# Gathered statistics of a second image spread over 60 attention units, and the second moments and tile mask split between the attention and the head of the convolution

## The reference

```python
x = x + _L0_conv_ref(_gn(x), W_qkv, W_out, rel_height, rel_width)  # window attention
x = x + _L1_conv_ref(_gn(x), weight, bias)                         # 3x3 convolution

def _gn(v, G=32, eps=1e-5):        # mean and variance over 4 channels and a whole image
    ...
    return ((g - m) / jnp.sqrt(s + eps)).reshape(v.shape)

def _L1_conv_ref(x, weight, bias):
    x_sp = x * _tile_mask(x)       # a 32x32 tile counts if any channel has |x| > 1e-6 in it
    y = conv 3x3 of x_sp, padding 1
    return y + bias
```

## Time and profile before

| | |
|---|---|
| median of 3 runs | 3703.85 us (3702.18 to 3705.59) |
| the profiled execution | 3702.19 us, span 3700.4 us, granted clock 0.991 |
| PE busy | 3491.4 us, 94% |
| DVE busy | 3349.1 us, 91% |
| ACT busy | 2966.0 us, 80% |
| POOL busy | 2575.1 us, 70% |
| DMA | 464.06 MB, mean 125 GB/s |

### The profile page before, as it was taken

The page is one execution under the profiler, slowest core; times in us unless marked ns, Lnnn a source line. Parts: engine busy times, 40 slices in busy tenths (PEclk is TensorE's granted clock), DMA queues, the critical chain, the costliest instruction groups (busy, mean ns, idle before and its releaser), DMA issues. The chain is left out here.

```text
span 3700.4 us, 127356 instructions
## 1 busy us (share of the span) xinstructions
PE 3491.4 (94%) x51718; PEld 2480.6 (67%) x51718; DVE 3349.1 (91%) x5626; ACT 2966.0 (80%) x5320; POOL 2575.1 (70%) x3344
## 2 busy tenths in 40 slices
PE   0799999998999999999999999999589999999999
PEld 0587777777888888888888888888434444444444
DVE  9699999999999999999999999999789888888887
ACT  0788888887999999999999999998377777777774
POOL 1677777776777777777777777777366666666664
PEclk9999999999999999999999999999799999999999
DMA  8244544443333333333333333333244434344332
GB/s 374 79 132 133 159 134 154 148 139 105 103 103 97 94 98 103 103 97 91 101 103 103 95 91 103 103 100 83 69 160 162 154 146 154 147 154 154 154 154 83
DMA packets 492549, 464.06 MB, mean 125 GB/s; under 512 B 9664, under 2 KB 469312, under 8 KB 469440
## 3 DMA queue, kind: packets, MB, share of 16 engines
q1 hardware_dynamic: 491968, 455.92, 38.4%
HBM read 321.40 MB, written 134.48 MB: 123 GB/s over the span
## 5 line engine op out<-in xcount | busy, mean ns | idle before, releaser
L984 POOL TENSOR_TENSOR sb_tf<-sb_cf 128x1024 f32<-128x1024 f32 x256 | 609.4, 2382 | 392.2 <-DVE sb_tl L966 370.3
L450 PE MATMUL ps_t<-sb_ident,sb_d 128*108 128x128 f32 x4096 | 662.3, 284 | 6.2 <-ACT sb_pt L638 1.9
L600 DVE TENSOR_TENSOR sb_qb<-ps_q,sb_own_head 128x1024 f32<-128x1024 f32 x512 | 621.1, 1213 | 14.9 <-PE ps_q L432 14.9
L470 PEld LDWEIGHTS ps_s<-sb_kf,sb_qb 128*64 128x64 f32 x16384 | 519.1, 138 | 171.5 <-issue 162.9
L719 POOL TENSOR_TENSOR sb_erel<-sb_brel 128x288 f32<-128x288 f32 x512 | 351.5, 686 | 395.6 <-DVE sb_brel L547 394.7
L892 PE MATMUL ps_c<-sb_th,sb_wc_h 128*128 128x512 f16 x1536 | 584.3, 380 | 40.3 <-DVE sb_tl L966 40.2
L470 PE MATMUL ps_s<-sb_kf,sb_qb 128*64 128x54 f32 x16384 | 585.6, 224 | 2.4 <-DVE sb_scores L580 2.4
L892 PE MATMUL ps_c<-sb_th,sb_wc_l 128*128 128x512 f16 x1536 | 583.3, 380 | 0.0
L892 PE MATMUL ps_c<-sb_tl,sb_wc_h 128*128 128x512 f16 x1536 | 583.2, 380 | 0.0
L749 POOL TENSOR_TENSOR sb_zl<-sb_zf,sb_zh 128x396 f16<-128x396 f32 x512 | 481.1, 940 | 83.1 <-ACT sb_zh L702 83.1
L735 POOL TENSOR_TENSOR sb_prod<-sb_rel,sb_shift 128x192 f32<-128x192 f32 x1024 | 502.1, 511 | 0.0
(11 more groups left out here) (117 smaller groups left out, 8228.0 us busy)
## 6 DMA issues: line engine op xcount, KB each, us to landing
sb_xb<-rows SPq DMA_DIRECT2D x128, 780.0 KB, 6.5
sb_xc<-x SPq DMA_DIRECT2D x64, 1280.0 KB, 5.4
sb_x<-rows SPq DMA_DIRECT2D x128, 512.0 KB, 4.1
x<-sb_x SPq DMA_DIRECT2D x128, 512.0 KB, 3.3
out<-sb_oc SPq DMA_DIRECT2D x64, 1024.0 KB, 3.9
sb_abuf<-rows SPq DMA_DIRECT2D x16, 2048.0 KB, 11.7
sb_st<-rows SPq DMA_DIRECT2D x32, 1024.0 KB, 9.3
sb_raw<-wconv SPq DMA_DIRECT2D x1, 576.0 KB, 3.7
```

The lines of the kernel that those rows point to most:

```text
L450: last = pe.transpose(ps_t[0:KV, wj * 128:(wj + 1) * 128], d[:, at:at + KV], ident[:])
L470: last = pe.matmul(s_at, qb[:, qc:qc + QB], kf[:, kc:kc + KR], start=True, stop=True)
L600: dve.tensor_tensor(view(qb, 0, 128, vh * QBW + p * NW * QB, [[QB, NW], [QN, HEADS], [1, QN]]), view(ps_q, 0, 128, 0, [[QN, NW], [0, HEADS ...
L984: pool.tensor_tensor(tf[:, k * TF:(k + 1) * TF], view(cf, 0, 128, c0 + ra * W, [[2 * W, PAIRROWS], [1, W]]), view(cf, 0, 128, c0 + rb * W, ...
```

## The change

Five things are done.

1. The strip of 8 rows of the second image becomes a half strip of 4 rows (512 KB), 64 in all. Units 0 to 3 take two halves each, units 4 to 59 one each. Their loads stand at the end of SP's body, and all their `bn_stats` (two a half) at the end of VectorE's g=3.
2. The moments of the second image of x are made at u=60 instead of u=38.
3. The second moments of the first image are made in the attention, at u=70, without the five steps for the edge tables, and its tile mask and row tables at u=71, with a `partition_all_reduce` on GpSimd at g=0.
4. The zero rows around x1 are stored by SP at u=4.
5. The two blocks between attention and convolution are gone. The second moments, mask and tables of the second image are made at the convolution's start, on VectorE, with one matmul, one square root and one all-reduce; ScalarE waits for the group step before its first strip, and for the tables before the first strip of the second image.

```diff
+            HALF = WS // 2 * W
+            HALVES = H * W // HALF
+            DOUBLE = 4
+
+            def gathered(u):
+
+                if 0 <= u < DOUBLE:
+                    return (2 * u, 2 * u + 1)
+                return (u + DOUBLE,) if DOUBLE <= u < HALVES - DOUBLE else ()
+
+            MOMENTS = {HALVES - DOUBLE: 1, UNITS // B + 6: 0}
+            MASK = UNITS // B + 7
...
# SP, body u
-                    if stat is not None:
-
-                        row = settled(sp, (stat[0] + STRIPS_1) * WS + PAD)
-                        sp.wait_ge(sem["st_used"], (stat[0] + 1) * PAR)
-                        sp.dma_start(st[:, h * STW:(h + 1) * STW],
-                                     x_in[:, bass.ds(row, WS), :].rearrange("p a b -> p (a b)")
-                                     ).then_inc(st_loaded[h], 16)
                     if on(u - 3, UNITS):
...
                         sp.dma_start(view(x1, 0, 128, r * WS * UW, [[UW, WS], [1, UW]]),
                                      x_in[:, bass.ds(row, WS),
                                           UW * r:UW * r + UW]).then_inc(xr_loaded[r], 16)
+                    for k in gathered(u):
+
+                        row = H + k * (WS // 2) + PAD
+                        if k >= 2:
+                            sp.wait_ge(sem["st_used"], 2 * (k - 1))
+                        sp.dma_start(st[:, k % 2 * HALF:(k % 2 + 1) * HALF],
+                                     x_in[:, row:row + WS // 2, :].rearrange("p a b -> p (a b)")
+                                     ).then_inc(st_loaded[k % 2], 16)
+                    if u == DOUBLE:
+
+                        sp.wait_ge(sem["zeroed"], 1)
+                        for row in (0, ROWS + 1):
+                            sp.dma_start(x1_dram[:, row:row + 1, :].rearrange("p a b -> p (a b)"), zrow[:]
+                                         ).then_inc(sem["edges"], 16)
...
# VectorE, body u, end of group g
-                        if stat is not None:
-                            if g != 1:
-                                stat_pieces(stat, h, (0, 4, 1, 2)[g], (1, 0, 1, 2)[g])
...
+                        if g == 3:
+                            for k in gathered(u):
+                                dve.wait_ge(st_loaded[k % 2], (k // 2 + 1) * 16)
+                                for c in range(2):
+                                    at = UNITS * 6 + (2 * k + c) * 6
+                                    dve.bn_stats(stats[:, at:at + 6],
+                                                 st[:, k % 2 * HALF + c * 512:k % 2 * HALF + (c + 1) * 512]
+                                                 ).then_inc(sem["st_used"], 1)
+                        if u in MOMENTS:
+                            b = MOMENTS[u]
+                            if g == 0:
+                                moments_sums(dve, link[b], (b,), gn_sem[b]["agg_done"])
+                            if g == 2:
+                                moments_tables(dve, link[b], (b,), gn_sem[b]["sqrt_done"], edges=(b == 1))
+                        if u == MASK and g == 0:
+                            tile_extremes(dve, link[0], 0)
+                            dve.tensor_copy(ext[1][:, 0:1], ext[0][:, 0:1]).then_inc(sem["tiles_done"], 1)
+                        if u == MASK and g == 2:
+                            row_tables(dve, link[0], 0, sem["all_tiles"])
...
# GpSimd, body u, end of group g
+                        if u == MASK and g == 0:
+                            pool.wait_ge(sem["tiles_done"], 1)
+                            pool.partition_all_reduce(tiles_of(tabs, 0), tiles_of(ext[0], 0), 128, RMAX
+                                                      ).then_inc(sem["all_tiles"], 1)
...
-        groupnorm_moments("gn1", (0, 1))
...
# convolution: SP no longer stores and waits for the zero rows; ScalarE
+                    if j + 2 == CSTRIPS // B:
+                        act.wait_ge(sem["step_done"], TABLE_STEPS)
...
+                act.wait_ge(sem["step_done"], GROUP_STEPS)
+                act.activation(gn[5][:, 1:2], gn[3][:, 1:2], ACT.Sqrt).then_inc(sem["sqrt_done"], 1)
# VectorE
+                link = linker(dve, sem["step_done"])
+                moments_sums(dve, link, (1,), sem["agg_done"])
                 for z in (th, tl):
...
+                moments_group(dve, link, (1,), ps_c, sem["sum_done"])
+                moments_tables(dve, link, (1,), sem["sqrt_done"], edges=False)
+                tile_extremes(dve, link, 1)
+                dve.tensor_copy(ext[1][:, 0:1], ext[0][:, 0:1]).then_inc(sem["tiles_done"], 1)
+                row_tables(dve, link, 1, sem["all_tiles"])
```

More of the change, by code:

```diff
@@ L161, in moments_tables, with tiles_of @@
                                               ALU.mult, ALU.mult))
+        ctab = sb("ctab", 3 * CSTRIPS * TC, F32)
+        dtab = sb("dtab", 3 * CSTRIPS * TC, F32)
+        nmean = sb("nmean", B, F32)
+        TR = ROWS // TILE
+        SPT = TILE // CROWS
+        ext = [sb(f"tile_ext{j}", TR * TC, F32) for j in range(2)]
+        tabs = sb("tile_abs", TR * TC, F32)
+        zrow = sb("zrow", W, F32)
+        def tiles_of(t, b):
+            return t[:, b * TR // B * TC:(b + 1) * TR // B * TC]
@@ new lines, in tile_extremes @@
+        def tile_extremes(dve, link, b):
+            hs, n = STRIPS // B, TR // B
+            for t, dst, op in ((tmax, ext[0], ALU.max), (tmin, ext[1], ALU.min)):
+                for h in range(2):
+                    link(dve.tensor_reduce(view(dst, 0, 128, b * n * TC + 4 * h, [[TC, n], [1, 4]]),
+                                           view(t, 0, 128, b * n * 8 * SPT + 4 * h, [[8 * SPT, n], [1, 4], [8, SPT]]),
+                                           AX.X, op))
+                part = tiles_of(dst, b)
+                link(dve.tensor_scalar(part, part, mean_t[:, b * hs:b * hs + 1],
+                                       rstd_t[:, STRIPS + b * hs:STRIPS + b * hs + 1], ALU.subtract, ALU.mult))
+            link(dve.scalar_tensor_tensor(tiles_of(ext[0], b), tiles_of(ext[1], b), -1.0, tiles_of(ext[0], b),
+                                          ALU.mult, ALU.max))
@@ L369, in units @@
                 for u in range(-3, UNITS + 4):
-                    body(u, u // 2, u % 4, some,
-                         (u - FIRST, (u - FIRST) // 2) if FIRST <= u < GN else None, u == GN)
+                    body(u, u // 2, u % 4, some)
             def z_at(z, slot, p, off, dims):
@@ L382, in _, with body @@
             def _(sp):
[L383 removed]
+                def body(u, s, slot, on):
                     h = slot % 2
@@ L425, in project @@
                     need(pe, sem["qb_done"], piece)
[L426 to L430, removed]
+                    if due is not None:
+                        pe.wait_ge(gn_sem[due]["agg_done"], 1)
+                        pe.matmul(ps_q[:, 0:2], gsum[:], aggr[:, 2 * due:2 * due + 2], start=True, stop=True
+                                  ).then_inc(gn_sem[due]["sum_done"], 1)
+                        pe.wait_ge(gn_sem[due]["step_done"], GROUP_STEPS)
                     for c, (z, w) in enumerate(PRODUCTS):
@@ L517, in _ @@
             def _(dve):
+                dve.memset(zrow[:], 0.0)
                 for slot in range(2):
@@ L522, in _, with body @@
                 last.then_inc(sem["zeroed"], 1)
[L523 to L535, removed]
+                link = [linker(dve, gn_sem[b]["step_done"]) for b in range(B)]
+                def body(u, s, slot, on):
                     h = slot % 2
@@ L877, in _ @@
             def _(pe):
+                pe.wait_ge(sem["agg_done"], 1)
+                pe.matmul(ps_c[:, 0:2], gsum[:], aggr[:, 2:4], start=True, stop=True).then_inc(sem["sum_done"], 1)
                 def body(j, t, slot, on):
```

132 lines of the change are left out of this document (45 added, 87 removed).

## The result

The changed kernel takes 3770.23 us in the median of 4 runs (3768.9 to 3772.79), against 3703.78 us for the kernel before (3702.18 to 3705.59): the ratio is 1.018, with a 95% interval of 1.0162 to 1.0198. It is slower, by 66.5 us. The prediction was 3751 us, in a range of 3698 to 3802. The profiled execution has a span of 3768.0 us against 3700.4, which is 67.6 us more.

A forecast was written before the change was run, and what follows sets the result against it. TensorE was taken to bound the convolution and set the attention's pace, VectorE binding units with four gathered bn_stats. Attention +76.2 us and head -29.3 gave +46.9, so 3751 us, range 3698 to 3802.

The forecast's parts named there:

- units 4 to 59: Attention: 56 units, each 1.64 us above TensorE's 19.31 because VectorE waits for the half strip; +91.8 us.
- units 0 to 2: Attention's start: two half strips each, but no x1 work yet on VectorE; +1.5 us for the three, between 0 and 7.
- u=70: Attention: first image's group sums, the second image's chain without the five edge-table steps; +7.2 us.
- u=71 and 72: Attention, forecast for u=71: mask, row tables and all-reduce of the first image; +4.9 us, between 3 and 10.
- what falls away: Attention: cost of the old placement, 8.3 us around u=38 and 32.2 us in units with four gathered bn_stats; -40.5 us.
- head: Stretch before the convolution: ScalarE starts to normalise 29.9 us earlier, all-reduce about 0.6 us late for tf; -29.3 us.
- The queue's order: SP's loads in the attention: half strip lands 5.7 us after L413's issue, VectorE stalls 2.35 us, a unit takes 20.95 us.
- the half strip is hidden: Rival, attention: the half strip lands early enough and the change is faster, 3659 to 3670 us; chance 0.13.
- GpSimd's next erel waits some 1.5 us for the all-reduce: Attention at u=71: GpSimd's delay from the mask's all-reduce, part of that unit's +4.9 us.
- The all-reduce ends about 0.6 us after GpSimd's first tf could start: Convolution's start: the second image's all-reduce delays GpSimd's tf by about 0.6 us, within the -29.3 us.
- the clock rival: Rival, attention: each stall drops TensorE's clock, a unit takes some 24.3 us, 3940 us in all; chance 0.04.
- the stalled case: Main case, attention: VectorE stalls for the half strip in every unit and the kernel is slower; chance 0.83 including rival 3.

The follow-up runs named there:

- e1: Changed kernel with the half strip's load moved ahead of the store and load of x1 in SP's body; 3671.71 us, ratio 0.9912 to the kernel before.
- e2: Changed kernel with the half strip's load left last in SP's body, but loading the next unit's half strip; 3672.2 us, ratio 0.9913 to the kernel before.
- e8: Changed kernel loading only half of each half strip (256 KB), the second bn_stats reading the first rows again; 3728.72 us.
- e4: Changed kernel with both new all-reduces replaced by a tensor_copy on GpSimd, leaving out the maximum over the channels; 3754.29 us.
- e5: Changed kernel with the old gathering: whole strips in units 6 to 37, second image's moments at unit 38; 3702.9 us, ratio 0.9999 to the kernel before.

## Why the prediction came out as it did

The direction and the mechanism of the attention were right; the price of the all-reduce was not, and the total was 19.2 us too low. Term by term, in us over 19.31 a unit, from the bn_stats rows:

| term | predicted | measured |
|---|---|---|
| units 4 to 59 | 91.8 | 1379.84 - 203.66 - 56 x 19.31 = 94.8 |
| unit 3 | 3.0 | 22.10 - 19.31 = 2.8 |
| units 0 to 2 (and all before body 3) | 1.5 | 181.56 - 177.63 = 3.9 |
| group sums at u=60 | 8.3 | 1426.12 - 1379.84 - 38.62 = 7.7 |
| u=70 | 7.2 | 1607.91 - 1580.63 - 19.31 = 8.0 |
| u=71 and 72 | 4.9 | 1659.04 - 1607.91 - 38.62 = 12.5 |
| what falls away | -40.5 | -40.5 |
| head | -29.3 | -21.9 |
| sum | 46.9 | 67.3 |

(The 0.3 us to the 67.6 of the spans lie in the units behind 73. The head is the span less the last bn_stats of x1, 3768.0 - 2732.34 after, and 3700.4 less the last pair of L592 before, which the trace has at 2642.87.)

**The queue's order.** This step was right in each of its parts. L413's issue behind the minimum reduce, VectorE's arrival (3.35 to 3.6 predicted, 3.45 seen), the landing (5.7 predicted, 5.8 seen on average), VectorE's own work from the landing to the next issue (15.25 and 15.17) and the period (20.95 and 21.00) all answer to rows, and e1, e2 and e8 show that the distance between issue and use is the cause. Single units scatter between 20.3 and 22.5 us; the forecast took them all alike, and why the landing is a microsecond later in some wasn't tried. That the mean came out right with them is in part luck. The rival that the half strip is hidden, for which the rule of the Trainium skill spoke (4.3 us for both loads together), did not come: the earliest landing was 5.15. The fixed cost in that rule of the Trainium skill is given for DMAs that GpSimd issues; here SP issues them.

**The step that was mis-sized** is "GpSimd's next erel waits some 1.5 us for the all-reduce" at u=71, and its sister in the head, "The all-reduce ends about 0.6 us after GpSimd's first tf could start". Both took the price of an all-reduce from the wait that stood behind it in the kernel before, 2.6 us of VectorE. That row shows how long VectorE waits for the result. It does not show how long GpSimd is gone. The first wait was 9.6 us instead of 1.5. In the head the all-reduce ended 1.0 us before tf could start, so by the forecast's reckoning it would have cost nothing there; it cost 7.3. The two terms came out 7.6 and 7.4 us too low, 15.0 of the 20.4 us by which the sum was off, and e4, which takes away the all-reduces alone, gives back 15.9 us.

Before, GpSimd's silence fell in a stretch in which it had nothing to do:

```profile
L819 POOLq MODIFY_POOL_CONFIG  x2: 11/11/11, 2660.9 to 2660.9; - x2
2666.77 0.72 POOL L819 PARTITION_ALL_REDUCE sb_tile_abs<-sb_tile_ext  x1 [36.85 <-issue]
2689.44 25.81 POOL L984 TENSOR_TENSOR sb_tf<-sb_cf 128x1024 f32<-128x1024 f32 x9 [21.94 <-ACT sb_cf L911]
```

Behind the old all-reduce tf waited for ScalarE until 2689 in any case, so the time after it could not be seen. The time ahead of it could: 5.9 us lie between the mark and the all-reduce, which starts 1.8 us after its input was ready at 2665.00. These 1.8 us are the greater part of the 2.6. The prediction used neither this mark nor the "issue" releaser of the 36.9 us.

The Trainium skill ("GPSIMD Engine Reference", section 2.1, Instruction dispatch) says that the first call of a freshly loaded kernel on GpSimd pays about 6 us for loading its code, and names MODIFY_POOL_CONFIG as the mark of it. The trace agrees for the way in: 5.7 us from the mark to the all-reduce at u=71, and 5.9 before. By that rule the prediction would have had the all-reduce 2.8 us late at u=71. The larger part, the 7.0 and 8.35 us of the way back, is seen in these runs only.

**The rest.** The start cost 2.4 us more than taken; e1 still has some of it, e5, which has no half strips there, does not (its body 3 stands at 176.77), and it was not tried alone. In the head about 1 us is left, and the rows say where: from its first matmul to its last the convolution takes 1000.6 us after, and 999.5 before (2695.22 to 3694.75). TensorE had been idle for 20.9 us ahead of it after, and for 40.2 before; it starts at the lower of its two levels (1.2 GHz) in both. The clock came back to 1.00 some 5.6 us after the first matmul, against 2.9 before. The first row is from TensorE's timeline before; the others are stretches as in the earlier trace rows, two before and three after:

```profile
2695.22 0.61 PE L892 MATMUL ps_c<-sb_th,sb_wc_h 128*128 128x512 f16 x1 [40.18 <-DVE sb_tl L966]
2695.00:2698.00 3.00, 2.78 (x7) 1.03 (x8) 2.97 (x2) 3.00 (x7) 3.00 (x2) 0.50 0.00 0
2698.00:2700.00 2.00, 2.00 (x10) 0.88 (x9) 0.47 (x1) 2.00 (x4) 2.00 (x1) 0.97 0.00 0
...
2761.00:2766.00 5.00, 4.24 (x11) 1.48 (x12) 3.97 (x2) 5.00 (x10) 5.00 (x2) 0.50 0.00 0
2766.00:2768.00 2.00, 2.00 (x8) 0.80 (x6) 0.96 (x1) 1.76 (x3) 2.00 (x2) 0.65 0.00 0
2768.00:2770.00 2.00, 2.00 (x11) 0.93 (x10) 1.97 (x2) 2.00 (x2) 2.00 (x1) 1.00 0.00 0
```

That the clock makes the remaining microsecond is argued, not shown.

The rival that each stall costs TensorE its clock is refuted by the 1.00 over units 4 to 59. The prediction's evidence against it was thinner than it says: in its unit from 843.67 TensorE's two idle stretches are 0.8 and 0.6 us, not 1 to 2. In units 4 to 59 of the changed kernel the longest is 1.9 us, and the clock stays. Two more slips changed nothing in the time. By the prediction's own terms unit 59 ends near 1375 us, not 1260 (1379.84 was measured). And the clock rival, at 3940 us, belongs to slower; the 0.83 given for slower holds only the stalled case.

## What to carry to other kernels

Where one engine issues all loads in an order written by hand, a load's issue time is set by the longest wait ahead of it in that list; find what releases that wait and how far behind it the consumer stands, and put a load that depends on nothing ahead of the waits or one turn early. Spreading work evenly gains only if it also keeps its lead: here the same bn_stats in the same place cost 95 us or nothing, by the place of one DMA.

The price of an instruction moved into a busy stretch is the time for which its engine is gone, before and after it, and not the wait of whoever uses its result. A cost that was hidden in a stretch of idleness is seen only in the gaps of that engine's own timeline.

## What the runs showed of the hardware

A `partition_all_reduce` on GpSimd that itself takes 0.54 us blocked GpSimd for 5.9 us before it and 7.0 us (in the attention) or 8.35 us (in the head, of which 7.3 on the path) after it, until the next ordinary tensor operation started. The time before it was hidden where GpSimd was idle: in the head the mark stands at 2736.4 and the all-reduce starts at 2747.08, right when its input is ready. The time after it was hidden only in the kernel before, where GpSimd's next work came late. The same maximum of flags over 128 channels and 64 tiles by one matmul with ones cost less: in the two places 12.4 us less for two all-reduces, in a kernel that was 17.1 us faster as a whole.

Half strips of 512 KB behind 512 KB of 512-byte rows landed 5.8 us after the first issue on average, between 5.15 and 7.3, and 256 KB in their place 0.7 us sooner.

Idle stretches of TensorE of up to 1.9 us, in units 4 to 59 of the changed kernel, left its clock at 1.00.
